# Adding the experts' rows by accumulating scatters into two DRAM tables, in place of a mask product, with the projection moved last

## The reference, cut to what matters

```python
probs = jax.nn.softmax(x @ Wr, axis=-1)
topw, topi = jax.lax.top_k(probs, K)                     # K = 4 of E = 32
topw = topw / jnp.sum(topw, axis=-1, keepdims=True)
shared = silu(x @ Wsg) * (x @ Wsu) @ Wsd
shared = shared * jax.nn.sigmoid(x @ Wse)
xe = jnp.zeros((E, CAP, h), x.dtype).at[sel, posc].add(x[tok] * valid[:, None])   # CAP = 32
g = silu(jnp.einsum('ech,ehf->ecf', xe, Wg))
u = jnp.einsum('ech,ehf->ecf', xe, Wu)
ye = jnp.einsum('ecf,efh->ech', g * u, Wd)               # F = 176, h = 256
y_pair = ye[sel, posc] * (w * valid)[:, None]
out = shared.at[tok].add(y_pair)
...
x = x + attention(xn) + out
```

## Time and profile before

| | us |
|---|---|
| median of three executions | 429.58 |
| the profiled execution | 429.21 |
| its span, first to last instruction | 426.8 |
| PE busy in the span | 419.8 (98%) |
| VectorE, ACT, POOL busy | 310.9, 247.5, 168.6 |
| PE's granted clock | 1.00 throughout |

### The profile page before, as it was taken

How to read it: one execution, slowest core, us unless ns; L and a number is a source line. 1 busy time by engine, 2 the same in 40 slices (tenths; PEclk the granted TensorE clock), 3 DMA queues, 4 the chain that set the end, 5 groups by cost and what they waited for, 6 DMA issues and landing times.

```text
span 426.8 us, 8853 instructions
## 1 busy us (share of the span) xinstructions
PE 419.8 (98%) x3070; PEld 377.2 (88%) x3070; DVE 310.9 (73%) x910; ACT 247.5 (58%) x671; POOL 168.6 (40%) x293
## 2 busy tenths in 40 slices
PE   8999999999999999999999999999999999999997
PEld 8788879999999999999999999999997777567797
DVE  5967575787787888787877767657689994688442
ACT  4666741887868788777867786434314622563120
POOL 3520002645554554554554530102077007699200
DMA  7800020501010101010000000000099942899002
GB/s 214 303 2 1 2 76 25 198 1 51 2 51 0 51 2 51 2 52 1 2 0 3 2 2 0 27 14 12 26 321 300 307 115 88 236 305 279 9 14 86
DMA packets 37754, 34.45 MB, mean 81 GB/s; under 512 B 2448, under 2 KB 35920, under 8 KB 37712
## 3 DMA queue, kind: packets, MB, share of 16 engines
q1 hardware_dynamic: 37328, 32.85, 26.2%
q0 software_dynamic: 384, 1.05, 0.8%
HBM read 31.80 MB, written 2.10 MB: 79 GB/s over the span
## 4 chain that ended last, share of the span: by engine, by line
PE 92%; DVE 5%; ACT 2%; issue 1%; POOL 0%; POOLq 0%; DVEq 0%
PE bank L945 21%; PE bank L947 21%; PE bank L946 21%; PE bank L1116 5%; PE bank L1128 3%; PE bank L1107 3%; PE bank L1350 2%; PE bank L1317 2%; PE bank L1361 2%; PE bank L1362 2%; PE bank L1158 2%; PE bank L1337 2%; DVE OS L1859 1%; PE bank L1022 1%; PE bank L1266 1%; DVE arena L1499 1%
## 5 line engine op out<-in xcount | busy, mean ns | idle before, releaser
L587 POOL TENSOR_TENSOR arena<-arena,rinv 128x384 f32<-128x384 f32 x64 | 52.9, 828 | 81.0 <-DVE rinv L1629 81.0
L945 PE MATMUL bank<-XTl,WA 128*128 128x512 f32 (+1 forms) x126 | 52.0, 412 | 0.9 <-DVE arena L1499 0.8
L947 PE MATMUL bank<-XTh,WA 128*128 128x512 f32 (+1 forms) x126 | 49.1, 390 | 0.0
L946 PE MATMUL bank<-XTh,WA 128*128 128x512 f32 (+1 forms) x126 | 49.1, 389 | 0.0
L771 ACT ACTIVATE PT<-bank 128x256 fp32r<-128x256 f32 x64 | 24.5, 383 | 34.0 <-PE bank L1116 34.0
L1633 DVE TENSOR_TENSOR PT<-bank,PT 128x256 fp32r<-128x256 f32 x64 | 27.2, 425 | 18.8 <-ACT arena L772 18.8
L945 PE MATMUL bank<-WA,XTh 128*128 128x256 f32 x128 | 38.3, 299 | 0.0
L578 POOL CAST Q<-arena 128x128 fp32r<-128x128 f32 x64 | 18.7, 292 | 47.0 <-PE bank L947 47.0
L946 PE MATMUL bank<-WA,XTl 128*128 128x256 f32 x128 | 35.7, 279 | 0.0
L947 PE MATMUL bank<-WA,XTh 128*128 128x256 f32 x128 | 35.7, 279 | 0.0
L1621 DVE CUSTOM_DVE_ANT_0 arena<-bank,posm 128x128 f32<-128x128 f32 x64 | 18.1, 283 | 20.8 <-PE bank L947 20.8
(11 more groups left out here) (329 smaller groups left out, 1455.5 us busy)
## 6 DMA issues: line engine op xcount, KB each, us to landing
arena<-in_L_ffn_Wg SPq DMA_DIRECT2D x6, 704.0 KB, 7.8
arena<-in_L_ffn_Wu SPq DMA_DIRECT2D x6, 704.0 KB, 10.3
arena<-in_L_ffn_Wd SPq DMA_DIRECT2D x6, 512.0 KB, 7.2
arena<-in_L_attn_Wk SPq DMA_DIRECT2D x8, 256.0 KB, 2.6
arena<-in_L_attn_Wv SPq DMA_DIRECT2D x8, 256.0 KB, 3.2
arena<-in_L_attn_Wo SPq DMA_DIRECT2D x1, 2048.0 KB, 8.4
arena<-in_L_ffn_Wd SPq DMA_DIRECT2D x6, 192.0 KB, 7.6
arena<-in_L_attn_Wq SPq DMA_DIRECT2D x4, 256.0 KB, 4.7
```

Source lines behind the costliest of these rows:

```text
L587: pool.tensor_tensor(pr, pr, r[:, :, None].to_broadcast([P, 3, P]), ALU.mult).then_inc(s_p, 1)
L945: pe.matmul(dst, wh, xl, start=start, stop=False)
L946: pe.matmul(dst, wl, xh, start=False, stop=False)
L947: return pe.matmul(dst, wh, xh, start=False, stop=stop)
```

## The change

- The mask product goes. In its place each group's weighted rows are first merged within the group: `SAME[g]` is a mask of 128 x 128, 1 where two slots of the group hold the same token. One float32 product of it with the weighted rows (`expert_merge`) gives each slot the sum over all slots of its token. The first slot of each token gets the token's row number, the others a spare row (`row_places`).
- POOL then adds the group's 128 rows to a DRAM table with an indirect DMA that accumulates (`scatter`). Groups 1, 3, 5 go to one table, the others to the second; a scatter waits until the one before it in its table has landed. Both tables are set to zero early, by two DMAs of 1.15 MB each.
- SP loads the tables back in four DMAs each; VectorE adds them to `X` (`add_rows`), POOL adds the second table for the first three tiles.
- The shared expert's tiles 5, 6 and 7 are moved behind `down` of group 7, and the projection becomes a last block of its own (`final_tile`), into eight banks.
- Of the probabilities x values, tiles 6 and 7 move from POOL to VectorE (`last_values`, 14 instructions).
- Expert weights are laid out on the host so that a partition's part of a group is one run (11,264 bytes for Wg and Wu together, half of that for one of the places, and 4,096 for Wd).

```diff
+                 ("turn", 0), ("slots", 3), ("up", 2), ("ranks", 0), ("down", 0), ("turn", 1), ("slots", 4), ("up", 3), ("merge", 0),
...
+                 ("split", 1), ("split", 2), ("sd", 2), ("merge", 2), ("split", 3), ("down", 3), ("up", 4), ("slots", 5), ("copy", 2), ("merge", 3),
...
+                 ("ao", 0), ("down", 7), ("ao", 1), ("merge", 7), ("copy", 7), ("sd", 5), ("sd", 6), ("sd", 7), ("add", 7)]
...
+PV_STEPS = [("values", 0), ("values", 1), ("values", 2), ("scatter", 0), ("values", 3), ("scatter", 1), ("values", 4), ("scatter", 2),
+            ("values", 5)] + [("scatter", g) for g in range(3, GR)]
+IN_FRONT = {2: 0, 3: 1, 4: 2, 5: 3, 6: 4, 7: 6}
+ON_POOL = 3
...
+            for table in expert_rows:
+                sp.dma_start(table.rearrange("(g p) d -> p g d", p=P), ZR[:, None, :].to_broadcast([P, GR + 1, D])).then_inc(s_xs, 16)
...
+                    sp.dma_start(part, a["experts_up"][g, :, m * h:m * h + m].rearrange("p e c n -> p (e c n)")).then_inc(s_ew[i], 16)
...
-            for j in range(NT):
-                sp.wait_ge(s_pa, j + 1)
+            for t, g in ((1, 5), (0, GR - 1)):
+                sp.wait_ge(s_xg[g], 32)
+                for k in range(B):
+                    sp.dma_start(YS[t][:, 2 * k:2 * k + 2], expert_rows[t][2 * P * k:2 * P * k + 2 * P].rearrange("(g p) d -> p g d", p=P)).then_inc((s_x, s_wq)[t][k], 16)
+            for j in range(ON_POOL, NT):
+                sp.wait_ge(s_pa, j - ON_POOL + 1)
                 sp.dma_start(out_t[:, j], X[:, j]).then_inc(s_out, 16)
+                if j < 2 * ON_POOL:
+                    sp.wait_ge(s_pv, 18 + j - ON_POOL + 1)
+                    sp.dma_start(out_t[:, j - ON_POOL], X[:, j - ON_POOL]).then_inc(s_out, 16)
...
+            def scatter(g):
+                if g == 0:
+                    pool.wait_ge(s_rk, 1)
+                if g in IN_FRONT:
+                    pool.wait_ge(s_xg[IN_FRONT[g]], 32)
+                pool.wait_ge(s_yr, g + 1)
+                pool.indirect_dma_start(expert_rows[int(g in (1, 3, 5))], bass.IndirectOffsetOnAxis(ap=rank[:, g:g + 1], axis=0), YZ[:, g], None,
+                                        compute_op=ALU.add).then_inc(s_xg[g], 16)
...
+            def y_weighted(g):
+                act.wait_ge(s_dn, g + 1)
+                act.wait_ge(s_sw1, 1)
+                if g >= 2:
+                    act.wait_ge(s_mg, g - 1)
+                nc.scalar.activation(YW[:, g % 2], pb[7][:, 0:D], ACT.Copy, scale=slot_w[:, g:g + 1]).then_inc(s_ye, 1)
+
+            def y_merged(g):
+                act.wait_ge(s_mg, g + 1)
+                nc.scalar.activation(YZ[:, g], pb[3][:, 0:D], ACT.Copy).then_inc(s_yr, 1)
...
+                for half in range(2):
+                    ins = pe.matmul(pb[4 + half][:], onesr[0:1, :], TKr[0:1, 512 * half:512 * half + 512], start=True, stop=True)
...
+            def expert_merge(g):
+                pe.wait_ge(s_ye, g + 1)
+                if g >= 1:
+                    pe.wait_ge(s_yr, g)
+                pe.matmul(pb[3][:, 0:D], SAME[:, g], YW[:, g % 2], start=True, stop=True).then_inc(s_mg, 1)
...
+            pe.wait_ge(s_pjl, 1)
+            pe.wait_ge(s_al, 4)
+            pe.wait_ge(s_ye, GR)
+            for j in range(NT):
+                if j == 5:
+                    pe.wait_ge(s_x2, NT - 1)
+                if j == 6:
+                    pe.wait_ge(s_yr, GR)
+                if j == 7:
+                    pe.wait_ge(s_x2, NT)
+                final_tile(j)
...
+            def add_rows(t, j):
+                dve.wait_ge((s_x, s_wq)[t][j // 2], 32)
+                ins = nc.vector.tensor_tensor(X[:, j], YS[t][:, j], X[:, j], ALU.add)
+                if t == 0:
+                    ins.then_inc(s_pa, 1)
+                else:
+                    step(ins)
...
+            for j in range(NT):
+                add_rows(1, j)
             for j in range(NT):
                 add_rest(j)
+            for j in range(ON_POOL, NT):
+                add_rows(0, j)
```

More of the change, by code:

```diff
@@ L243, in program @@
         pvt = sb("pvt", [P, 256])
-        s_x = [sem(f"x_loaded{b}") for b in range(B)]
+        onesr = sb("onesr", [1, P], FR)
+        spare = sb("spare", [P, 1])
+        earlier = sb("earlier", [P, GR])
+        slot_d = sb("slot_d", [P, GR])
+        rank = sb("rank", [P, GR], U32)
+        expert_rows = [nc.dram_tensor(f"expert_rows{t}", (N + P, D), F32, kind="Internal").ap() for t in range(2)]
+        s_x = [sem(f"x_then_expert_rows_loaded{b}") for b in range(B)]
         s_xb0 = sem("x_second_tile_loaded")
@@ L624, in _ @@
                 pool.indirect_dma_start(XG[:, g], None, rows, bass.IndirectOffsetOnAxis(ap=idx[:, g:g + 1], axis=0)).then_inc(s_xg[g], 16)
[L625 to L632, removed]
+            pool.wait_ge(s_gt, 2)
@@ L633, in _, with values @@
+            pool.affine_select(out=BEFORE, in_=SAME, compare_op=ALU.is_gt, fill=0.0, base=0,
+                               pattern=[[0, GR], [-1, P]], channel_multiplier=1).then_inc(s_it, 1)
+            chain = [0]
+            def values(j):
+                pool.wait_ge(s_ap, 1)
+                for k in range(j // 2 + 1):
+                    p, v = value_operands(j, k)
                     dst = AO[:, j] if k == 0 else pvt[:]
                     pool.tensor_tensor(dst.rearrange("p (g r d) -> p g r d", g=G1, r=4), p, v, ALU.mult).then_inc(s_pv, 1)
-                    chain += 1
@@ L643, in _ @@
+            for what, n in PV_STEPS:
+                if what == "values":
+                    values(n)
+                if what == "scatter":
+                    scatter(n)
+            for j in range(ON_POOL):
+                pool.wait_ge(s_x[j // 2], 32)
+                pool.wait_ge(s_pd, 2 + j + 1)
+                pool.tensor_tensor(X[:, j], YS[0][:, j], X[:, j], ALU.add).then_inc(s_pv, 1)
         @block.scalar
@@ L925, in _ @@
                     nc.scalar.activation(ACTh[:, n - 1], ACTT[n - 1][:, N // 2:N], ACT.Copy).then_inc(s_adh, 1)
-                if what == "high":
-                    if n == 0:
[L928 to L937, removed]
-                nc.scalar.activation(AOTh[:, f // 2, 512 * (f % 2):512 * (f % 2) + 512], pb[4 + f][:], ACT.Copy).then_inc(s_ac, 1)
+                if what == "down":
+                    y_weighted(n)
+                if what == "copy":
+                    y_merged(n)
+                if what == "ao":
+                    if n == 0:
+                        nc.scalar.activation(PJh[:], projT[:], ACT.Copy).then_inc(s_pjh, 1)
+                    for c in range(C):
+                        act.wait_ge(s_at, 2 * n + c + 1)
+                        nc.scalar.activation(AOTh[:, c, 512 * n:512 * n + 512], pb[ao_bank(c, n)][:], ACT.Copy).then_inc(s_ac, 1)
         @block.tensor
@@ L1874, in _ @@
                     shared_product(n[0])
+                if what == "shared" and n == (11, 1):
+                    same_token(0)
+                    same_token(1)
                 if what == "table":
@@ L1899, in _ @@
                     scores_weighed(1)
-                if what == "mask":
-                    for g in n:
-                        dve.wait_ge(s_it, 4)
-                        slot_mask(g)
-                if what == "low":
-                    for g in range(n, n + 3):
-                        y_low(g)
                 if what == "sd" and n >= 1:
```

235 lines of the change are left out of this document (125 added, 110 removed).

## The result

| | before | after |
|---|---|---|
| median, us | 429.76 (429.38 to 429.99, 4 runs) | 424.78 (424.4 to 425.91, 4 runs) |
| the profiled execution | 429.21 | 424.53 |
| its span | 426.8 | 422.8 |
| last product of PE starts | 423.88 | 414.67 |
| from there to the end of the span | 2.9 | 8.1 |

The ratio is 0.9889, with a 95% interval of 0.9868 to 0.991: faster by 1.1%. The median before has one execution more than the 429.58 further up. The forecast was 424.3, with a range of 420.8 to 428.6.

The account below looks back on a forecast made before the run. PE's products were taken to bound the last 60 us. PE's sum -11.6, merge waits +1.9 and tail +4.4 gave -5.3 us: profiled 429.21 to 423.9, plus 0.4 to the median, 424.3; range 420.8 to 428.6.

Parts of the forecast that it names:

- PE's sum: PE's products: 15.2 us removed, 3.5 for merges and 0.5 for spreading added; with waits, PE ends 9.7 us earlier.
- The waits: PE standing at merges 3, 5 and 6 for ACT: 1.9 us in sum, bounds 0 and 4.
- The wait at merge 3: At group 3's merge PE waits 1.2 us for ACT, whose work there includes a table load.
- The tail: After PE's end, VectorE's serial additions, then stores: 7.2 us to the span's end, was 2.8; gives back 4.4.
- the stores: Eight stores on SP at the end, allowed 0.4 us each; the seven after the first start over 2.8 us.
- The scatters: Accumulating DMAs to the tables: 4.5 us each, bounds 1.7 and 10; hidden with 2 to 5 us to spare.
- rival 1: At the kernel's end the scatters end last because accumulates are slow: 432.3 us with 11 us each; chance 0.11.
- Rival 3: In the tail, VectorE's eight additions stretch to about 0.9 us beside active POOL, 3.9 more: 428.2; chance 0.15.
- Rival 4: Late expert weights at 250 GB/s make `up` 7 wait about 2 us: 426; chance 0.10.
- Rival 2: PE's gain arrives whole: ACT ahead at the merges, tail at its lower bound: 421.5; chance 0.14.

Follow-up runs that it names:

- e1: The kernel before with only the routed experts' weights laid out and loaded in long runs: 429.62 us, ratio 1.0001 to the kernel before.
- e2: The changed kernel with the weights' old layout and short-run loads: 424.65 us, ratio 0.9901 to the kernel before.
- e3: The changed kernel with ACT's copy of merged block 2 moved ahead of its work on the following tiles: 423.31 us, ratio 0.9872.
- e5: The changed kernel with all eight scatters in one table, each waiting for the one before: 433.22 us, ratio 1.0094.
- e6: The changed kernel with shared tiles 5 to 7 and their additions put ahead of `down` 6: 428.5 us, ratio 0.9978.
- v1: The changed kernel with block 2's copy early, table 1's additions shared between POOL and VectorE's gap, tiles 0 to 2 stored first: 420.62 us, ratio 0.9816.
- e8: The changed kernel with tiles 0 to 2 stored from ACT's queue, the rest from SP's: 423.92 us, ratio 0.988.
- e7: The changed kernel with the eight merges as single fp32r products, merged rows losing low bits: 423.01 us, ratio 0.9849.

## Why the prediction was right, point by point

- **PE's sum.** Forecast 9.7 us earlier, measured 9.2 (414.67 + 0.12 against 424.0). Two terms were short. The eight merges take 4.4 us in the chain (0.63, 0.43, 0.43, 0.67, 0.43, 0.70, 0.70, 0.43), not 3.5: the three behind a stand take 0.67 or 0.70, and merge 0, before which no wait is listed, 0.63. The waits are 1.3 at merge 3 and about 0.5 and 0.3 at 5 and 6 (from the first transpose of `turn` to the merge it is 0.78 and 0.58 us, and the transposes themselves take 0.27): 2.1 for my 1.9. With both the sum would be 8.5 earlier. Two terms that I didn't have make up for them. The 128 mix products filled 15.8 us from start to start and not 15.2, since one next to a float32 product takes about 0.2 us instead of 0.12. And in the kernel before PE lost 0.5 us between the start of `up` of group 1 and the transposes of group 0. PE's own wait list doesn't show it, but its weight loads stood there for 0.7 us until VectorE's product L1886 was done. `up` in the kernel before, then in the changed one:

```profile
362.96 1.73 PE L1317 MATMUL bank<-arena 128*32 128x352 f32 x16
363.60 1.39 PE L1377 MATMUL bank<-arena 128*32 128x352 f32 x16
```

  The transpose behind it starts at 364.79 and 364.92, so the piece went from 1.83 to 1.32 us. e1 has the loss too (1.76 busy) and e2 hasn't (1.39); which part of the change took it away is not shown. With these two the sum is 9.6 earlier, and 0.4 us stays open. One reading was wrong without harm: PE's longest wait after 320 us is 0.7 us, for ACT's L827 near 323, and not 0.4. The changed kernel has the same wait.
- **The wait at merge 3.** Place, cause (the table load) and size (1.2) held, and e3 shows that its removal is worth the whole of it and, besides, the 0.24 us that a merge takes longer behind a stand.
- **The tail.** VectorE's additions came at 3.64 and 3.25 us where 3.7 and 3.4 stood. They began 0.7 later (409.77 for 409.1), 0.5 of it with PE, and the first store went out 0.6 late. The term that was mis-sized is the stores: 0.4 us each was my allowance from 0.33, a duration of stores that nothing was queued behind, and in a row they take 0.5, which is 0.6 us over seven of them. From PE's end to the end of the span it is 8.0 and not 7.2.
- **What made up for it.** The span came out 1.3 longer than forecast (422.8 against 421.5), but only 1.7 us lay around it instead of the 2.4 that I carried over. That 424.3 is nearer to 424.78 than its parts were is luck.
- **The scatters.** 4.5 us by gather plus store, 4.3 measured once the weights are there. Beside the weights' loads it was 9.0, near my upper bound, and I had given one price for both. In the changed kernel that costs nothing, as only early scatters meet the loads, and rival 1 stayed away: POOL and VectorE waited for no rows. e5 shows that in one chain it makes the kernel slower than before, and e6 that the room was 2.0 us, the lower edge of my 2 to 5.
- **Rival 3** fell for the changed kernel: L1941 took 416 to 427 ns in all 13 cases. Its condition, POOL adding at the same time, was not met there; v1 met it and paid up to 1.5 us for one addition. That GpSimd shares its SBUF interfaces with VectorE's instructions with two SBUF inputs, as the Trainium skill says (GPSIMD Engine Reference, Specifications), agrees with 0.42 alone and 1.96 beside POOL. It showed in the changed kernel as well, at the first `last_values`: from 389 to 391 us, with POOL's own products running, two of the fourteen took 0.76 and 0.84 us instead of 0.42, and PE did not wait for them. That `add_rest` and POOL's 0.74 did not disturb each other agrees too.
- **Rival 4** fell, with e1 and e2: neither the old nor the new runs of weights were waited for. Rival 2 was right that the waits could be avoided, and wrong that they would be.

## What to carry to other kernels

When a merge or a copy on a second engine stands between two products of the first, walk the second engine's order at each of them; the one with a table load in front was worth 1.7 us of span and one moved tuple. After products are taken away, price the tail as a queue of its own: serial additions, then stores at the spacing of a full queue and not at the duration of a single one. A chain of accumulating DMAs is to be priced in the traffic that it meets, and split over tables if it must start early.

## What the runs showed of the hardware that I had not expected

- An accumulating scatter of 128 rows of 1 KB took 3.8 to 4.3 us from issue to landing after the weights' loads, and 9.0 to 10.3 beside them (scatter 0 of the changed kernel, e5 and e6, with 331 to 355 GB/s on the core's DMAs). It takes POOL 1.6 us to issue, against 0.95 for a gather.
- Stores queued behind each other on SP are mostly issued 0.5 us apart, where a single one shows 0.33. With three of the eight moved to ACT's queue, SP's five still went 0.47 apart (e8).
- A float32 product of 256 columns takes 0.43 us in the stream and 0.67 to 0.70 behind a stand; in fp32r (e7) it is 0.12 and 0.36 to 0.39. Here the stand cost 0.24 to 0.27 us more, nearly what the second pass costs (0.31).
- Seven times fewer packets for the same bytes changed neither the time of the kernel nor the waits of PE (e1, e2).
